# A gated cross-attention block with a token mix on one core: centred first embedding, late token mix, values split ahead

## The reference

```python
xn  = layernorm(x)                      # per token, no gain
emb = xn + ctx
q, k, v = emb @ wq + bq, emb @ wk + bk, emb @ wv + bv
ek  = exp(k - max_t k)                  # maximum over the tokens of the element
ew  = exp(w - max_t w)                  # w = pos_bias inside |t - j| < 64, else 0
y   = sigmoid(q) * (ew @ (ek * v)) / (ew @ ek)
a   = layernorm(y @ wo + bo + emb) * gamma + beta
o   = layernorm(relu(a @ w1 + b1) @ w2 + b2 + a) * gamma + beta
x1  = x + tanh(g_x) * o
z   = layernorm(x1); zp = z shifted by one token (first one 0)
xr  = mu_r * z + (1 - mu_r) * zp;  xk = mu_k * z + (1 - mu_k) * zp
out = x1 + tanh(g_f) * sigmoid(xr @ Wr) * (relu(xk @ Wk)**2 @ Wv)
```

## Time and profile before

| | us |
|---|---|
| median of 3 runs (lowest, highest) | 459.3 (458.5, 459.55) |
| the profiled execution's own time | 458.91 |
| its span in the trace | 457.1 |
| PE busy | 435.7 (95%) |
| DVE busy | 380.0 (83%) |
| ACT busy, POOL busy | 286.0, 286.1 (63% each) |

### The profile page before, as it was taken

One profiled execution on the slowest core, in us unless ns is written; L12 is line 12 of the kernel. 1 busy time (PEld: TensorE's weight loads), 2 busy tenths in 40 slices (PEclk: granted clock), 3 DMA queues, 4 the chain that ended last, 5 costly groups with the idle time before them and its releaser, 6 DMA issues.

```text
span 457.1 us, 8142 instructions
## 1 busy us (share of the span) xinstructions
PE 435.7 (95%) x2892; PEld 394.4 (86%) x2892; DVE 380.0 (83%) x768; ACT 286.0 (63%) x449; POOL 286.1 (63%) x227
## 2 busy tenths in 40 slices
PE   8989989997999999999999999999999999998975
PEld 8778789996988888998889888998889898987975
DVE  4998869987597979799798979799788876598887
ACT  3683563835687578745967487745965478537453
POOL 2586847571878657894878657894868453753611
PEclk9999999999899999999999999999999999999999
DMA  8840330442215750448215650445213330011002
GB/s 275 280 138 2 106 103 2 129 125 81 93 55 169 190 150 5 138 128 208 92 56 170 189 145 9 139 127 162 95 58 122 102 101 1 0 48 46 3 0 93
DMA packets 43497, 47.23 MB, mean 103 GB/s; under 512 B 8512, under 2 KB 39744, under 8 KB 43456
## 3 DMA queue, kind: packets, MB, share of 16 engines
q1 hardware_dynamic: 42368, 45.13, 32.6%
q10 hardware_dynamic: 1088, 1.57, 1.0%
HBM read 30.76 MB, written 15.93 MB: 102 GB/s over the span
## 4 chain that ended last, share of the span: by engine, by line
POOL 33%; issue 28%; DVE 15%; PE 11%; ACT 10%; DMA 2%; SPq 0%; POOLq 0%; DVEq 0%; ACTq 0%
PE ps L1806 10%; POOL ek_lo L240 5%; POOL ev_lo L240 5%; POOL x_beta L626 3%; POOL xk_lo L240 2%; POOL emb L352 2%; POOL a_rows L626 2%; POOL rs_mid L618 2%; POOL rs_fin L618 2%; POOL nmr_fin L621 1%; POOL rs_ff L618 1%; DVE ps L948 1%; DVE xk L1031 1%; DVE xr L1031 1%; POOL rs_head L618 1%
## 5 line engine op out<-in xcount | busy, mean ns | idle before, releaser
L1806 PE MATMUL ps<-w_hi,hid_hi 128*128 128x256 f32 x248 | 62.2, 286 | 0.8 <-issue 0.5
L1806 PE MATMUL ps<-w_lo,hid_hi 128*128 128x256 f32 x248 | 61.7, 285 | 0.0
L1595 ACT ACTIVATE hid_hi<-ps,b 128x512 fp32r<-128x512 f32 x60 | 37.7, 681 | 23.6 <-PE ps L1806 23.6
L1806 PE MATMUL ps<-a_hi,w_hi 128*128 128x512 f32 x128 | 50.9, 397 | 1.1 <-DVE hid_lo L1108 1.1
L240 POOL TENSOR_TENSOR ek_lo<-y,ek_hi 128x1024 fp32r<-128x1024 f32 x13 | 36.2, 2788 | 24.5 <-DVE xr L1031 17.8
L1806 PE MATMUL ps<-a_hi,w_lo 128*128 128x512 f32 x128 | 50.7, 396 | 0.0
L1806 PEld LDWEIGHTS ps<-w_hi,hid_hi 128*128 128x128 f32 x248 | 47.6, 192 | 1.7 <-issue 1.2
L1806 PEld LDWEIGHTS ps<-w_lo,hid_hi 128*128 128x128 f32 x248 | 47.5, 192 | 0.3
L1108 DVE SCALAR_TENSOR_TENSOR hid_lo<-ps,neg_b,hid 128x512 fp32r<-128x512 f32 x60 | 41.3, 736 | 3.2 <-ACT hid L1601 3.2
L1601 ACT ACTIVATE hid<-hid_hi,neg_b 128x512 f32<-128x512 f32 x60 | 40.0, 722 | 0.0
L240 POOL TENSOR_TENSOR ev_lo<-res,ev_hi 128x1024 fp32r<-128x1024 f32 x8 | 19.1, 2392 | 29.7 <-ACT ev_hi L1509 29.7
(11 more groups left out here) (278 smaller groups left out, 1407.8 us busy)
## 6 DMA issues: line engine op xcount, KB each, us to landing
x_in<-in_x SPq DMA_DIRECT2D x8, 512.0 KB, 4.6
emb<-in_ctx SPq DMA_DIRECT2D x8, 512.0 KB, 4.3
x_beta<-in_x SPq DMA_DIRECT2D x8, 512.0 KB, 4.3
out<-out_sb SPq DMA_DIRECT2D x7, 512.0 KB, 4.3
key_room<-norm SPq DMA_DIRECT2D x6, 512.0 KB, 2.6
y<-key_room SPq DMA_DIRECT2D x24, 128.0 KB, 2.9
fin_room<-xk SPq DMA_DIRECT2D x6, 512.0 KB, 2.6
out_sb<-fin_room SPq DMA_DIRECT2D x24, 128.0 KB, 2.9
```

What stands on the lines that cost most here:

```text
L1595: act.activation(tile(hi, b, T), bank(relu_pair(n, q), b), ACT.Relu, bias=b1[:, m:m + 1]).then_inc(hid_hi_done, 1)
L1806: return pe.matmul(o, s, m, start=start, stop=stop, skip_group_check=True)
```

## The change

Eight things are edited.

1. The first x is loaded in two halves, one on SyncE's queue and one on ScalarE's (`first_x`).
2. The first embedding is made from centred x: VectorE subtracts the mean while GpSimd computes the scale, and one instruction for each tile multiplies by the scale and adds the context. ScalarE's two tiles and the two additions are gone. GpSimd forms the power ahead of the shift.
3. Head orders: `unit_low(1)` goes from VectorE to GpSimd, behind the masking, which now waits for `emb_done`; the first queries use pair 0 in place of pair 3, and their Exp comes behind the position table's.
4. First denominator: `weigh_values(0)` goes ahead of the far low part on VectorE; on TensorE all of chunk 0, then the wait for `far_lo_done`, then chunk 1, then both small products. `ev_high(0)` goes ahead of `tile_rows`, and on GpSimd `ev_low(0)` ahead of `make_emb(1)`.
5. `turn_emb(1, 1)` goes behind the whole numerator; `sums_high(0, 1)` goes ahead of `emb_high(1)`.
6. Values split ahead: at the end of step 1 ScalarE does `ev_high(2)` ahead of `normalise("fin", 0)`, GpSimd does `ev_low(2)` between the `ff` and `fin` statistics, and VectorE does `finish_x1(0)` ahead of `sums_low(2, 0)` and `hidden_low(1, 0)`.
7. In step 7 `finish_a(7)` waits for the output of element 5 (`out_done`).
8. Late token mix: ScalarE writes (1 - mu) * z, shifted, for k and r from PSUM (`last_prev_k`, `last_prev_r`), and VectorE adds mu * z from PSUM to it (`last_mix`), with no difference. The order is k of both halves ahead of r; `xr`'s second low half goes to GpSimd, `last_keys(1)` goes ahead of `last_gates(0)`, and element 6's `make_out` goes behind the last low part.

```diff
@@ -397,7 +400,17 @@
-        last_delta_t, last_xk_t, last_xr_t, last_y = hid[0], hid[1], gate_q, y
+        last_xk_t, last_xr_t, last_y = hid[1], gate_q, y
+        prev_r_rows = (a_rows[BATCH % 2], hid[0])
+        def prev_k(h, c, shift):
+            return xn_half(h, shift)[:, c]
+        def prev_r(h, c, shift):
+            return prev_r_rows[c][:, 2 * P * h + shift:2 * P * (h + 1) + shift]
@@ -451,6 +464,11 @@
+        def first_x(eng, h, landed):
+            eng.dma_start(half(x_in, h).rearrange("p (b a d) -> p b a d", b=1, a=TT // 2),
+                          rows_of(A_x, 0)[:, :, 2 * h:2 * h + 2]).then_inc(landed, 16)
@@ -620,6 +638,18 @@
+            def first_head_stats():
+                mvs = mv["head"].rearrange("p (a s) -> p s a", s=2)
+                pool.wait_ge(mv_done["head"], TT)
+                pool.tensor_tensor(ve["head"], mvs[:, 1], eps_col, ALU.add).then_inc(ve_done["head"], 1)
+                pool.wait_ge(ve_done["head"], 1)
+                pool.tensor_tensor(rs["head"], ve["head"], minus_half, ALU.pow).then_inc(rs_done["head"], 1)
+                pool.tensor_tensor(nm["head"], mvs[:, 0], minus_one, ALU.mult).then_inc(ve_done["head"], 1)
+                pool.wait_ge(ve_done["head"], VE["head"])
+                pool.wait_ge(rs_done["head"], 1)
+                pool.tensor_tensor(nmr["head"], nm["head"], rs["head"], ALU.mult).then_inc(nmr_done["head"], 1)
@@ -665,8 +695,8 @@
             pool.wait_ge(ident_set, 5)
-            stats("head", 0)
-            pool.wait_ge(w_lo_done[0], 1)
+            first_head_stats()
+            pool.wait_ge(emb_done, 1)
@@ -676,6 +706,7 @@
                                    pattern=[[-P, 2], [1, T]], channel_multiplier=-1).then_inc(pos_masked, 1)
+            unit_low(1)
@@ -683,8 +714,8 @@
             emb_plus_bo(0, 0)
+            ev_low(0)
             make_emb(pool, 1, 1)
-            ev_low(0)
@@ -715,6 +746,7 @@
                 stats("ff", b)
+                ev_low(d)
@@ -744,6 +777,7 @@
                 if is_last(i):
+                    pool.wait_ge(out_done, i - 1)
@@ -778,6 +812,8 @@
             last_stats("fin", 1)
+            pool.wait_ge(xr_hi_done, BATCH + 1)
+            pool.tensor_tensor(half(xr_lo, 1), half(last_xr_t, 1), f32(half(xr_hi, 1)), ALU.subtract).then_inc(last_xr_lo, 1)
@@ -1113,19 +1149,28 @@
             dve.memset(xn_t[:, T + 1:T + 2], 0.0).then_inc(const_set, 1)
-            head_stats(0)
-
-            dve.wait_ge(nmr_done["head"], 1)
-            normalise_tiles("head", x_in, range(TT - FIRST_DVE, TT))
+            for h, landed in enumerate((x_landed, x_half_landed)):
+                dve.wait_ge(landed, 16)
+                for a in range(2 * h, 2 * h + 2):
+                    dve.bn_stats(tile(st["head"], a, HD), tile(x_in, a)).then_inc(st_done["head"], 1)
+            dve.wait_ge(st_done["head"], TT)
+            dve.memset(held, 0.0)
+            for a in range(TT):
+                dve.bn_aggr(tile(mv["head"], a, 2), tile(st["head"], a, HD)).then_inc(mv_done["head"], 1)
+            dve.wait_ge(mv_done["head"], TT)
+            for a in range(TT):
+                dve.tensor_scalar(tile(x_in, a), tile(x_in, a), mv["head"][:, 2 * a:2 * a + 1], None, ALU.subtract
+                                  ).then_inc(norm_done["head"], 1)
             dve.wait_ge(ctx_landed, 16)
-            dve.wait_ge(norm_done["head"], TT)
-            for h in range(2):
-                v = tile(emb[0], h, 2 * D)
-                dve.tensor_tensor(v, tile(x_in, h, 2 * D), v, ALU.add
-                                  ).then_inc(*((emb_half_done, 1) if h == 0 else (emb_done, 1)))
+            dve.wait_ge(rs_done["head"], 1)
+            for a in range(TT):
+                dve.wait_ge(norm_done["head"], a + 1)
+                dve.scalar_tensor_tensor(out=tile(emb[0], a), in0=tile(x_in, a), scalar=rs["head"][:, a:a + 1],
+                                         in1=tile(emb[0], a), op0=ALU.mult, op1=ALU.add
+                                         ).then_inc(*((emb_tile_done, 1) if a < TT - 1 else (emb_done, 1)))
...
             emb_low(0)
-            unit_low(1)
@@ -1139,10 +1184,10 @@
+            weigh_values(0)
...
-            weigh_values(0)
@@ -1196,9 +1241,9 @@
                 weigh_values(d)
+                finish_x1(b)
...
                 hidden_low(i, 0)
-                finish_x1(b)
@@ -1319,34 +1364,29 @@
-            def last_difference(h):
-                dve.wait_ge(xn_t_done, DC * (BATCH - 1) + h + 1)
+            def last_mix(dst, mu, prev, h, ready, done):
+                dve.wait_ge(ready, DC * (h + 1))
+                for c in range(DC):
+                    dve.scalar_tensor_tensor(out=chunk(dst, h, c), in0=tile(bank(3, h), c),
+                                             scalar=vec[:, mu + c:mu + c + 1], in1=prev(h, c, 0), op0=ALU.mult, op1=ALU.add
+                                             ).then_inc(done, 1)
+            def last_mix_k(h):
                 dve.wait_ge(hid_lo_done, 2 * NQ * BATCH)
-                dve.tensor_tensor(half(last_delta_t, h).rearrange("p (c t) -> p c t", c=DC), xn_half(h, 1), xn_half(h, 0),
-                                  ALU.subtract).then_inc(delta_done, 1)
-
-            def last_mix(dst, mu, h, done):
-                dve.wait_ge(delta_done, h + 1)
-                for c in range(DC):
-                    dve.scalar_tensor_tensor(out=chunk(dst, h, c), in0=chunk(last_delta_t, h, c),
-                                             scalar=vec[:, mu + c:mu + c + 1], in1=xn_half(h, 0)[:, c], op0=ALU.mult, op1=ALU.add
-                                             ).then_inc(done, 1)
-
-            def last_mix_k(h):
-                last_mix(last_xk_t, C_MUK, h, xk_done)
+                last_mix(last_xk_t, C_MUK, prev_k, h, prev_k_done, xk_done)
...
                 dve.wait_ge(den_read, DC * BATCH)
-                last_mix(last_xr_t, C_MUR, h, xr_done)
+                last_mix(last_xr_t, C_MUR, prev_r, h, prev_r_done, xr_done)
...
-            def last_xr_low(h):
-                dve.wait_ge(xr_hi_done, BATCH + h)
-                dve.tensor_tensor(half(xr_lo, h), half(last_xr_t, h), f32(half(xr_hi, h)), ALU.subtract
+            def last_xr_low():
+                dve.wait_ge(xr_hi_done, BATCH)
+                dve.tensor_tensor(half(xr_lo, 0), half(last_xr_t, 0), f32(half(xr_hi, 0)), ALU.subtract
@@ -1373,6 +1413,8 @@
             last_fin_stats(0)
+            for ap in prev_r_rows:
+                dve.memset(ap[:, 0:1], 0.0).then_inc(prev_zero, 1)
@@ -1380,24 +1422,21 @@
             last_fin_stats(1)
-            last_difference(0)
+            last_mix_k(0)
             last_normalise(1)
-            last_mix_k(0)
+            last_xk_low(0)
             sq_low(dve, a)
-            last_xk_low(0)
+            last_mix_k(1)
             last_mix_r(0)
-            last_difference(1)
-            last_mix_k(1)
-            last_xr_low(0)
...
             last_mix_r(1)
+            last_xr_low()
             last_square(0)
-            last_xr_low(1)
+            last_square(1)
             gate_ffn(a)
-            last_square(1)
-            make_out(a)
...
             dve.tensor_tensor(half(sq_lo, 1), half(last_xk_t, 1), f32(half(sq_hi, 1)), ALU.subtract).then_inc(last_sq_lo, 1)
+            make_out(a)
@@ -1603,17 +1642,16 @@
+            first_x(act, 1, x_half_landed)
...
             act.wait_ge(x_landed, 16)
+            act.wait_ge(x_half_landed, 16)
...
             load_unit(act, 1)
-            act.wait_ge(nmr_done["head"], 1)
-            for a in range(TT - FIRST_DVE):
-                normalise_tile("head", x_in, a)
@@ -1629,10 +1667,10 @@
                     exp_keys(0)
-                    act.wait_ge(act_const, 1)
-                    exp_q(0, 3)
...
             act.activation(c_col, pos_nmax, ACT.Exp).then_inc(c_col_done, 1)
+            act.wait_ge(act_const, 1)
+            exp_q(0, 0)
@@ -1641,12 +1679,12 @@
             normalise("head", 1, x_in)
+            ev_high(0)
             act.activation(tile_rows, far_in[:, 0:TT * FAR], ACT.Copy).then_inc(tile_rows_done, 1)
-            ev_high(0)
...
             unit_high(3)
+            sums_high(0, 1)
             emb_high(1)
-            sums_high(0, 1)
@@ -1680,11 +1718,11 @@
                 choose_log()
+                sums_high(d, 0)
                 hidden_high(i, 0)
-                sums_high(d, 0)
                 hidden_high(i, 1)
+                ev_high(d)
                 normalise("fin", b, x1)
-                ev_high(d)
@@ -1746,10 +1784,19 @@
-            def last_turned_copy(h):
+            def last_prev_k(h):
...
                 act.wait_ge(fin_turned, DC * (BATCH - 1) + h + 1)
-                act.activation(xn_half(h, 1), bank(3, h).rearrange("p (c t) -> p c t", c=DC), ACT.Copy).then_inc(xn_t_done, 1)
+                for c in range(DC):
+                    k = C_MUK - C_MUR + c
```

(48 more changed lines are left out.)

25 lines of the change are left out of this document (16 added, 9 removed).

## The result

| | before | after |
|---|---|---|
| median of the runs, us | 459.3 | 463.15 |
| lowest and highest of 4 runs | 458.5, 459.55 | 460.84, 467.07 |
| profiled execution, its span | 458.91, 457.1 | 462.72, 460.9 |
| mean granted clock of that execution | 0.996 | 0.981 |

The change makes the kernel slower: 1.0091 times the time before, 95% interval 1.0053 to 1.0129, and outside the predicted range. The runs also spread over 6 us where those of the kernel before spread over 1, and the slower ones have the lower mean clock (0.988 at 460.84, 0.969 at 467.07).

A forecast was written before the change was run, and what follows sets the result against it. TensorE was taken to set the pace, with VectorE's list ending last in the tail. Terms 2.8 + 1.0 + 0.4 - 1.1 - 1.9 = +1.2 us, shaded to +0.9, gave 460.2 us; own range 459.2 to 461.2, 8 in 10 from 457.0 to 461.9.

The forecast's parts named there:

- edits 1 to 3, to E: Head, up to the end of the keys' high part: an earlier embedding and no wait before the table's turn, 0.9 us gained.
- edit 4, first denominator: First attention: the denominator's first half comes after chunk 1's band products, 1.5 us later against the keys' high part.
- edit 5, the turn in the open: Behind the first numerator: the next embedding's turn and copy, hidden before, now delay the next keys; costs 2.2 us.
- y's low part beside GpSimd: Head, after the numerator: y's split and GpSimd's low part fit under 4.6 us of products, so no cost.
- the clock in the head: After the new stand of 3.4 us TensorE's clock falls to 0.50 for 3 us, partly during another wait: +1.0 us.
- edit 6, step 2: Step 2: the wait before the values is replaced by one of 3.7 us, with a clock fall behind it: +0.4 us net.
- edit 7, step 7: Step 7: VectorE's output no longer overlaps GpSimd's `finish_a`, and TensorE's wait of 1.09 us goes: -1.1 us.
- edit 8, tail: Tail: VectorE loses two differences and one low half, three at 0.6 to 0.7 us: -1.9 us.
- Rival (a): The clock holds in the head: 459.5 us, or 458.0 if it holds in step 2 also; chance 0.22.
- (b): Head: the denominator doesn't hold VectorE, so the 0.9 us carry through: 458.0, or 456.5 if step 2 keeps its clock; chance 0.19.
- (d): Head: GpSimd's masking and low part end after TensorE wants the values, the 0.9 us aren't gained: 461.0 us; chance 0.08.
- (c): Tail: ScalarE's some 2 us more of copies bound it, so edit 8 gives 0: 462.1 us; chance 0.09.

The follow-up runs named there:

- e11_after_filled: Changed kernel, orders kept, with 12 identity products in the first numerator's stand and 4 in the wait for the next embedding's high part: 459.29 us, 1.0010.
- e2_filler: Changed kernel with 14 more identity products on TensorE in the stand before the first numerator's chunk 1: 459.83 us, 1.0011.
- e4_before_45: Kernel before with edits 4 and 5 alone: 467.79 us, 1.0176.
- e1_no45: Changed kernel with edits 4 and 5 undone, edits 1 to 3 and 6 to 8 kept: 455.45 us, 0.9908.
- e7_before_8: Kernel before with edit 8 alone, the late token mix and the tail's new order: 458.53 us, 0.9981.
- e12: Kernel of e11_after_filled with ScalarE's high part of y moved ahead of the raw embedding's copy and two weight units: 462.36 us, 1.0074.
- e10: Kernel of e9 with 7 identity products in TensorE's tail wait of 1.98 us, before element 6's last product: 453.43 us, 0.9876.
- e3: Changed kernel with edit 5 alone undone, edit 4 kept: 457.21 us, 0.9952.
- e9: Kernel of e1_no45 with step 2's second sums split earlier on ScalarE and VectorE: 453.31 us, 0.9879.

## Why the prediction was wrong

The sign was right, and so was the main mechanism: the stand, the turn in the open and a fall of the clock all came. The time was 3 us too low. By its own steps, in the traces:

| step | predicted | measured |
|---|---|---|
| edits 1 to 3, to E | -0.9 | -1.4 |
| edit 4, first denominator | +1.5 | +1.5 |
| edit 5, the turn in the open | +2.2 | +2.1 |
| y's low part beside GpSimd | 0 | +1.2 |
| **the clock in the head** | **+1.0** | **+4.3** |
| edit 6, step 2 | +0.4 | -0.7 |
| edit 7, step 7 | -1.1 | -2.0 |
| edit 8, tail | -1.9 | -1.3 |

The measured column adds up to +3.7; the spans differ by 3.8. Apart from the clock, the errors run both ways and come to -0.8 us together; that they nearly cancel is luck. The clock's part and the two above it are e11_after_filled's: its next keys start 2.1 us later than before against the numerator's chunk 1 (38.83 from 34.73, 36.62 from 34.66), and mid 0 comes 8.4 us behind them for 7.2.

**The step that failed is the clock's price.** The prediction took one fall of 3 us at 0.50 from the earlier trace rows and set off a part of it against the wait for the embedding's copy. In the profile after, one fall lasts from about 33.4 to 40.3 us and a second from 43.7 to 50.5. The first is longer than the one priced; behind that wait, put down as a discount, came the second. Whether the wait brought it on isn't shown: e2_filler leaves that gap open, and its median is within 0.6 us of e11_after_filled's; and in the traces of e2_filler and e4_before_45 the same wait has no fall behind it. e11_after_filled, which changes no order and fills both gaps, puts the clock at 4.3 us in the traces and 3.9 in the medians. The trace of e4_before_45 has the same stand at a price of 1.4, inside the prediction's bounds. So the price is not one number: it went from 1.4 to 4.3 us for the same stand. The bound of 1.5 took one row of 3 us for the longest that a fall can last. Other rows show some 3 us at a stand of 3.29 (before), 7 at 3.85 (e1_no45), none at the same 3.29 (e7_before_8, where the stretch from 110 to 130 us has 1.00).

**The orders.** Against E the first `gate_den` starts at +5.04 where +5.1 was worked out, and the second sums are at 34.24 with E at 23.99, 1.5 later against E than before: this part was right to a tenth. The turn in the open was right also. What was overlooked stands behind it: the sentence that y's split and GpSimd's low part "fit under the 4.6 us of products" counted durations, not places in the lists. On ScalarE `y_high` stands behind the next embedding's copy and two weight units, all of which wait for the turn; it ran at 43.96 for 39.89. VectorE's low part, at 45.05, then fell beside the second of GpSimd's two low parts there, that of a weight unit:

```profile
42.26 2.38 POOL L243 TENSOR_TENSOR emb_lo<-xk,emb_hi 128x1024 fp32r<-128x1024 f32 x1 [9.83 <-ACT xk L1688]
44.59 2.37 POOL L675 TENSOR_TENSOR w_lo<-x,w_hi 128x1024 fp32r<-128x1024 f32 x1
```

It took 3.00 us for the 1.23 that it takes alone in the kernel before (at 40.98). The Trainium skill (SBUF — State Buffer, SBUF: two separate sides) says that a VectorE instruction with two inputs from SBUF and a GpSimd instruction that reads SBUF exclude each other for the whole of one of them. The traces agree: 3.00 to 3.03 us beside GpSimd, 1.23 without, and 3.35 against 1.29 for `make_out`; in the rows here GpSimd's ends at 44.59 + 2.37 = 46.96, and VectorE's ends 1.1 us later.

**Edit 6** was mis-sized within its bounds: the new stand is 3.85 us (3.7 predicted), and what the clock does at it varies by more than the edit is worth. **Edit 7** gave VectorE's whole 2.06 us, where only TensorE's wait had been counted; that is outside its bound of 1.5. **Edit 8** gave 1.3 where the clock held in the tail (32.2 in the traces of after, e11 and e12, and in e10 with its wait filled) and next to nothing where it fell there (33.7 in e1, e2 and e3, 33.5 in e7, 33.2 in e9). The five traces without edit 8 all have 33.5 or 33.6, with a wait of 1.5 to 1.8 us and no fall at it. The change made that wait 1.98, where the 1.74 of before had been read as safe.

Rival (a), that the clock holds, is what e11_after_filled makes by hand, and its time there, 459.29, is near the 459.5 given; in part by luck, since the 1.2 us of y's low part are in the one and not in the other. Rivals (b) and (d) are excluded by the rows of VectorE. Of (c) the part holds that VectorE waits for ScalarE, but in e7_before_8 it does so behind a TensorE at half clock.

What stays open is why a fall comes in one execution and not in the next with the same waits, and how long it lasts: the runs show only that both vary.
